# Two small tables ahead of the input in SBUF: the same program with ten tiles 96 bytes later

## The reference

```python
x = x + attn0(cond0(x, cond_8))        # per-sequence 256x256 weights, then 2-head causal attention with RoPE
x = x + ffn0(cond2_0(x, cond_8))       # SwiGLU of the picked expert (512), then top-2 of 8 experts, capacity 640
x = x + attn1(cond1(x, cond_8))        # 2 picked + 1 shared gated MLP (1024), then a minGRU scan
x = x + ffn1(cond2_1(x, cond_8))       # base + LoRA projection, then ternary-weight MLP (1024)
```

```python
g = einsum('bsh,hi->bsi', x, gate_w); u = einsum('bsh,hi->bsi', x, up_w)
return einsum('bsi,ih->bsh', gelu(g) * u, down_w)
```

## The kernel before

| Tile | Bytes per partition | Begins, modulo 128, before |
|---|---|---|
| residual, input_hi, input_lo | 16384 each | 0 |
| weight_stage | 24640 | 0 |
| identity and five more constants | 512, 256 (four), 512 | 64 |
| mlp_hi, mlp_lo, hidden_hi and hidden_lo of the MLPs | 24576 and 2048 | 96 |
| ternary weights, last hidden tiles, expert weights, inputs and hidden tiles | | 96 |
| folded_hi and folded_lo, gru and adapted weights, first_half_swapped | | 96 |
| expert0_hi and expert0_lo of the first batch | 12288 each | 96 |
| expert0_hi and expert0_lo of the second batch | 12288 each | 0 |
| hidden_hi and hidden_lo of the SwiGLU | 8192 | 32 |
| out_weights_hi, out_weights_lo | 2048 | 0 |

## Time and profile before

### The profile page before, as it was taken

How to read it: one execution, slowest core, us unless ns; L and a number is a source line. 1 busy time by engine, 2 the same in 40 slices (tenths; PEclk the granted TensorE clock), 3 DMA queues, 4 the chain that set the end, 5 groups by cost and what they waited for, 6 DMA issues and landing times.

```text
span 954.5 us, 13194 instructions
## 1 busy us (share of the span) xinstructions
PE 937.9 (98%) x4895; PEld 779.0 (82%) x4895; DVE 527.7 (55%) x972; ACT 447.3 (47%) x831; POOL 268.8 (28%) x243
## 2 busy tenths in 40 slices
PE   8999999999999999999999999999999999999998
PEld 4768868878799999998888888888888888888786
DVE  6754453685657666685564564334333335687544
ACT  3656565423255455573343353353342343345775
POOL 1533221300366765563310153041140230010000
PEclk9999999999999999999999999999999999999999
DMA  8030001202436443432503003003003012000011
GB/s 297 24 122 18 18 1 67 78 28 100 107 89 150 156 129 129 122 111 76 179 23 133 23 23 133 1 0 133 1 1 133 0 39 94 1 1 1 0 45 45
DMA packets 22193, 67.49 MB, mean 71 GB/s; under 512 B 4514, under 2 KB 11954, under 8 KB 19314
## 3 DMA queue, kind: packets, MB, share of 16 engines
q1 hardware_dynamic: 16546, 40.15, 11.5%
q0 software_dynamic: 5440, 26.50, 9.5%
q10 hardware_dynamic: 144, 0.00, 0.0%
HBM read 55.09 MB, written 9.45 MB: 68 GB/s over the span
## 4 chain that ended last, share of the span: by engine, by line
PE 91%; DVE 4%; issue 2%; ACT 1%; DMA 1%; POOL 0%; SPq 0%; ACTq 0%; DVEq 0%; POOLq 0%
PE banks L1087 20%; PE banks L1089 19%; PE banks L1088 19%; PE banks L1320 5%; PE banks L1321 5%; PE banks L1322 5%; PE banks L1179 3%; PE banks L1163 2%; PE banks L1372 2%; PE banks L1371 2%; PE banks L1170 1%; PE banks L1358 1%; PE banks L1359 1%; PE banks L1247 1%; DMA weight_stage<-in_cond_w 1%
## 5 line engine op out<-in xcount | busy, mean ns | idle before, releaser
L1087 PE MATMUL banks<-input_hi,mlp_hi 128*128 128x512 f32 x376 | 149.6, 398 | 0.0
L1089 PE MATMUL banks<-input_hi,mlp_lo 128*128 128x512 f32 x376 | 149.4, 397 | 0.0
L1088 PE MATMUL banks<-input_lo,mlp_hi 128*128 128x512 f32 x376 | 148.9, 396 | 0.0
L1582 ACT CAST hidden_hi<-hidden 128x512 fp32r<-128x512 f32 x96 | 59.6, 621 | 165.4 <-DVE hidden L1987 111.3
L2177 POOL TENSOR_TENSOR mlp_lo<-weight_stage,mlp_hi 128x768 fp32r<-128x768 f32 x32 | 59.0, 1842 | 179.2 <-ACT mlp_hi L1556 179.2
L1993 DVE TENSOR_TENSOR hidden_lo<-hidden,hidden_hi 128x512 fp32r<-128x512 f32 x96 | 66.4, 692 | 62.0 <-ACT hidden_hi L1582 60.3
L1987 DVE SCALAR_TENSOR_TENSOR hidden<-banks,L_expert_weight,gelu 128x512 f32<-128x512 f32 x64 | 48.1, 751 | 90.8 <-PE banks L1089 88.0
L1576 ACT ACTIVATE gelu<-banks 128x512 f32<-128x512 f32 x96 | 57.6, 600 | 68.0 <-PE banks L1089 67.9
L1088 PEld LDWEIGHTS banks<-input_lo,mlp_hi 128*128 128x128 f32 x376 | 71.0, 189 | 16.2
L1089 PEld LDWEIGHTS banks<-input_hi,mlp_lo 128*128 128x128 f32 x376 | 70.7, 188 | 16.6
L1087 PEld LDWEIGHTS banks<-input_hi,mlp_hi 128*128 128x128 f32 x376 | 70.6, 188 | 16.2
(11 more groups left out here) (333 smaller groups left out, 2176.7 us busy)
## 6 DMA issues: line engine op xcount, KB each, us to landing
weight_stage<-in_packF SPq DMA_DIRECT2D x8, 1536.0 KB, 7.8
weight_stage<-in_shared SPq DMA_DIRECT2D x2, 3072.0 KB, 10.1
expert_output<-y_rows SPq DMA_DIRECT2D x40, 128.0 KB
weight_stage<-in_cond_w SPq DMA_DIRECT2D x4, 512.0 KB, 5.5
residual<-in_xT SPq DMA_DIRECT2D x4, 512.0 KB, 10.8
first_half_swapped<-first_half SPq DMA_DIRECT2D x16, 128.0 KB, 2.1
routed_input<-x_rows SPq DMA_DIRECT2D x16, 128.0 KB, 1.7
weight_stage<-in_ffn_w SPq DMA_DIRECT2D x2, 1024.0 KB, 8.9
```

Of the source, the lines that this page charges most:

```text
L1087: pe.matmul(o, wh, dh, start=(i == 0), stop=False)
L1088: pe.matmul(o, wh, dl, start=False, stop=False)
L1089: last = pe.matmul(o, wl, dh, start=False, stop=(i == len(terms) - 1))
L1582: act.copy(hiD[n % 4][:, :], prod_t[n % 2][:, :]).then_inc(done)
```

## The change

Two small tables, `rev` (32 bytes of each partition) and `cond` (64 bytes), are allocated ahead of the residual and not behind the constants.

```diff
+    rev = sb("eight_minus_expert", [P, G])
+    cond = sb("conditioning", [P, B, G])
     xT = sb("residual", [P, KD, N])
     inH = sb("input_hi", [P, KD, N], F32R)
     inL = sb("input_lo", [P, KD, N], F32R)
@@
     ones16 = sb("ones_bf16", [P, P], BF16)
     ones32 = sb("ones", [P, P])
-    rev = sb("eight_minus_expert", [P, G])
-    cond = sb("conditioning", [P, B, G])
     dyn0 = sb("rows_of_L0_cond2", [P, B], I32)
```

## The result

The changed kernel takes 939.5 us in the median (939.34 to 939.60, 4 runs); the kernel before 951.01 us (950.27 to 951.25, 4 runs). The ratio is 0.9879, 95% interval [0.9868, 0.9891]: 11.5 us faster, where 6.4 were forecast. The time lies under the range of 941.5 to 949.7 us.

A forecast was written before the change was run, and what follows sets the result against it. PE was taken as the bound, through the distance between matmul starts. Gains of 5.95 us outside attention, 0.3 in attention and 0.2 in the ternary layer made 6.4: 951.24 - 6.4 = 944.8 us, range 941.5 to 949.7.

The forecast's parts named there:

- main term: Matmuls streaming the input outside attention: 1488 at 4 ns less each, 5.95 us gained; bounds 2.6 to 8.8 us.
- the hidden groups change although none of their tiles moved: Sign of a wrong forecast in the MLPs: something else sets the distance; the forecast had hidden groups staying at 392 ns.
- A price per matmul and not per column: SwiGLU at 256 columns and MLPs at 512: the same step, read as 4 ns per matmul whatever the width.
- The ternary layer: 128 matmuls on the input there: 1.5 ns less each, 0.2 us gained.
- The pair of the SwiGLU: SwiGLU down projection, two sequences: 4 ns more where the streamed tile begins at 0 than at 96.
- the SwiGLU and attention: Input matmuls in these stages: 0.8 us gained in SwiGLU and routing, 0.3 us in attention.
- The rival of no effect: Whole kernel: the address doesn't matter, the input is slower by its place in the loop; 951.2 us, chance 0.12.
- The collision rival: Input products: both PE reads at the same place collide, 1632 matmuls lose 5 ns, 8.2 us; 959.4 us, chance 0.05.
- DMA: Rival on the 8.12 us step into weight_stage: off-boundary writes take twice as long, 8.1 us more; 952.9 us, chance 0.03.
- The identity's 1.1 us either way: 265 matmuls streaming the identity, moved from 64 to 32: 1.1 us gained or lost, counted as zero.
- The wait and the low clock near 262 us: PE's 1.8 us wait, then 3.4 us at 1.2 GHz: between 1.3 us lost and 3.5 us gained, kept as is.

The follow-up runs named there:

- the input alone: Kernel before with only input_hi and input_lo moved to 96 modulo 128, residual and weight_stage left at 0: 943.91 us, ratio 0.9864.
- the map: Matmuls on PE alone, reference computation left out, for all 64 pairs of streamed and loaded starts: 226.8 to 234.3 ns at 512 columns.
- second profile of the kernel before: The kernel before profiled once more, nothing changed: span 950.1 us, without the 1.8 us wait and the low clock.
- 32 bytes: Kernel before with only the table of 32 bytes ahead of the residual, so the input begins at 32 modulo 128: 955.71 us, ratio 0.9992.
- everything at a multiple of 128: Kernel before with the input untouched and the tiles behind it moved to 0 modulo 128: 954.75 us, ratio 0.9980.

## Why the prediction was wrong

**The bound and the sign were right.** PE sets the time, the change acts through the distance between starts, the input's matmuls become faster, and nothing else becomes late: the stage of the MLPs shortened by what its matmuls gained, and the input alone gives all of it.

**The step that failed is the size of the main term, 4 ns per matmul on the input.** I took the hidden tiles as the measure of an undisturbed stream, "exactly the combination in which the hidden tiles run". Their combination was the good one, but their 230.0 ns were not its price: they ran behind twelve matmuls of the bad one and carried its slower step for three matmuls. The price is 226.7 ns, 7.5 under the 234.2 of the input's starts. So the input gained 6.6 ns on average and not 4 (7.5 us and not 4.6 in the MLPs), and the hidden tiles, which I had left out of the sum, gained 2.5 ns each, 1.5 us. By the map's prices of undisturbed streams alone, 7.5 ns on 1152 matmuls are 8.6 of the 8.96 us. The text said what would show it: "the hidden groups change although none of their tiles moved". My own held a warning: two equal combinations at 391 and 395 ns can't both be a price of the place.

**A price per matmul and not per column** was wrong as well. PE alone has 7.5 ns between the best and the dearest difference at 512 columns (226.8 and 234.3), 3.4 at 384 (173.3 and 176.7), and at 256 equal places are no gain. The pair at 256 columns could say nothing of the step at 512; that both gave 4 ns was chance.

**The ternary layer** was forecast at 1.5 ns per matmul on the input, 0.2 us. It gave 1.10 us: by the distances between starts 0.4 us on the input (3.0 ns each), 0.6 us on the hidden tiles and 0.1 us on matmuls of the LoRA projection that run among them. The hidden tiles, whose are at 391 and 395 ns, gained more than the input; that they had carried the input's slower step, as in the MLPs, fits this but was not tested alone. The four groups at 391 to 395 ns all went to 389.

**The pair of the SwiGLU** The earlier trace rows misled me about the cause. I read "the streamed tile begins at 0" out of a step of 4 ns between the two sequences. In the changed kernel the step is all but gone, though none of those tiles moved. The same groups there, first those that answer to the earlier trace rows:

```profile
L1087 PE MATMUL banks<-expert_hi,hidden_hi 128*128 128x256 f32 x32 | 9.2, 286 | 0.5 <-DVE x_rows L1794 0.5
...
L1088 PE MATMUL banks<-expert_lo,hidden_hi 128*128 128x256 f32 x32 | 9.0, 280 | 0.0
```

then those that answer to the earlier trace rows:

```profile
L1087 PE MATMUL banks<-expert_hi,hidden_hi 128*128 128x256 f32 x32 | 9.2, 287 | 0.0
...
L1088 PE MATMUL banks<-expert_lo,hidden_hi 128*128 128x256 f32 x32 | 9.0, 280 | 0.0
```

The first sequence's groups rose by 3 ns, where the text said that they "keep 283 and 277". So the pair was no price of the tile's place. The 96 distances between starts in the first sequence's down projection show two values for one pair of starts: 73 of them are 113 or 114 ns in the kernel before and most of the others 116 to 119, while in the changed kernel only 15 are 113 or 114, and 40 in a second profile of the changed kernel. What sets them stays open, and so does whether the layout has a part in it. With the difference of starts modulo 256 as the rule, the SwiGLU and attention give less than I summed, because out_weights and the second sequence's weights lie at 0 modulo 256 and the change takes the input from one bad difference to another, and the first sequence's down projection lost 0.3 us: 0.46 us where I had 1.1.

**The rival of no effect** drew on two pages of the Trainium skill. "SBUF — State Buffer", section "Specifications (TRN2)", with lines of 16 bytes, doesn't account for a period of 256 bytes. "TensorE: Matmul & The Clock Gate", section "Wait — 56ns, not 53.3ns?", gives N / 2.4 + 2.5 ns between starts, 215.7 ns at 512 columns; no pair of starts reached it here, the best was 226.6.

**The collision rival** was wrong at 512 columns and right in kind at 256: there equal places are among the dear ones, by up to 3 ns in the mean of a difference, and the experts' tiles gained 3 ns from being apart.

**DMA**: the transfer of 128 KB into weight_stage at its new place still lands after 2.1 us, and the chain's DMA step went from 8.12 to:

```profile
3.14 8.29 DMA weight_stage<-in_cond_w
```

0.17 us more, and scatter: the same step took 8.65 us in the second profile of the kernel before, and 7.90 to 8.77 us over all profiles of this program. The first stage as a whole was 0.36 us shorter than in that second profile. A cost of 0.2 us, as the prediction estimated it, can't be seen in such scatter. The identity's 1.1 us either way didn't come: the groups stayed at 274 ns.

**The wait and the low clock near 262 us** The earlier trace rows came and went without regard to the places of the tiles, as the section on the result shows. I had left them as they were. Their price was too low: at most 3.5 us by the sum of wait and slow stretch, and the two profiles of the kernel before differ by 4.8 us in that stage.

## What to carry to other kernels

Where PE streams float32 rounded operands back to back at 512 columns, put the streamed and the loaded tiles at the same start modulo 256. At 256 columns put them apart, by 192 as here; not every difference helps, 96 was no better than equal places (120.0 and 119.5 ns). And read the distance between starts, not the duration. Never take a tile's time in a mixed loop as its undisturbed time: a disturbed neighbour makes it dearer, so the gain of curing one is larger than their difference. A short loop on one engine over all pairs of starts settled what the edits of the full kernel beside it (32 bytes, everything at a multiple of 128) left ambiguous.

## What the runs showed that I had not expected

- The distance between matmuls of 512 columns depends on the difference of their two operands' starts modulo 256 bytes: 226.8 ns at 0, 229.2 at 64, 233.0 to 234.3 at the others. What makes these steps is not settled.
- After the operands agree again, the slower step lasts for three more matmuls (231 to 233, then 227 ns).
- With every product of the last three stages at the same place, nine in ten distances between matmuls of 512 columns are 226 or 227 ns.
- At 256 columns one difference, 192, settled at 113.4 ns in three pairs and at 117.8 in five of one run of PE alone, and one pair of starts took both kinds of value in the full kernel. What decides between them stays open.
